# Attention with conditioned queries and keys on one core: how the quarters of the key sums are added

## The reference

```python
Q, K, V = heads(x @ Wq.T + bq), heads(x @ Wk.T + bk), heads(x @ Wv.T + bv)
tQ, tK  = heads(tokens @ Wq.T + bq), heads(tokens @ Wk.T + bk)
scores  = einsum('bhqd,bhkd->bhqk', Q + tQ, K + tK) / sqrt(32)
attn    = softmax(scores, axis=-1)
out     = x + merge(einsum('bhqk,bhkd->bhqd', attn, V))
```

## Time and profile before

| | us |
|---|---|
| median of 3 runs | 686.24 (685.55 to 686.38) |
| the profiled execution, its own time | 690.45 |
| its span, first to last instruction | 688.7 |
| PE busy in the span | 667.9 |
| DVE busy | 541.5 |
| POOL busy | 490.5 |
| ACT busy | 375.3 |

### The profile page before, as it was taken

One profiled execution on the slowest core, in us unless ns is written; L12 is line 12 of the kernel. 1 busy time (PEld: TensorE's weight loads), 2 busy tenths in 40 slices (PEclk: granted clock), 3 DMA queues, 4 the chain that ended last, 5 costly groups with the idle time before them and its releaser, 6 DMA issues.

```text
span 688.7 us, 10047 instructions
## 1 busy us (share of the span) xinstructions
PE 667.9 (97%) x3528; PEld 451.3 (66%) x3528; DVE 541.5 (79%) x818; ACT 375.3 (54%) x659; POOL 490.5 (71%) x205
## 2 busy tenths in 40 slices
PE   6899999999999999999999999999999999999986
PEld 4677766666776666677666666776666677665421
DVE  4386788888888888888888888888888888888736
ACT  6325655555565555565555565555555556556452
POOL 5506777788777778877777887777778776667780
PEclk9899999999999999999999999999999999999787
DMA  7924345553434555343455543434554333444111
GB/s 230 244 53 102 88 115 138 139 135 98 116 100 109 138 138 140 101 115 100 102 138 140 138 115 102 110 94 136 139 139 122 82 101 93 113 124 124 32 48 46
DMA packets 48274, 79.85 MB, mean 116 GB/s; under 512 B 9824, under 2 KB 9824, under 8 KB 48224
## 3 DMA queue, kind: packets, MB, share of 16 engines
q1 hardware_dynamic: 48224, 79.21, 43.2%
HBM read 19.95 MB, written 8.39 MB: 41 GB/s over the span
## 4 chain that ended last, share of the span: by engine, by line
PE 89%; DVE 3%; DMA 2%; issue 2%; SPq 1%; POOL 1%; POOLq 1%; ACT 1%; DVEq 0%; ACTq 0%
PE bank L193 24%; PE bank L262 18%; PE bank L277 17%; PE bank L292 15%; PE bank L240 13%; DVE mf L520 1%; PE bank L300 1%; DMA Ks<-lo 1%; DMA xr<-xT 1%; DVE part_sums L533 1%; POOL A L670 1%; POOLq L40 1%; DMA Pt<-xT 1%; PE bank L309 1%; SPq L722 1%
## 5 line engine op out<-in xcount | busy, mean ns | idle before, releaser
L439 ACT ACTIVATE Pt<-bank 128x512 f32<-128x512 f32 x512 | 301.2, 598 | 240.1 <-PE bank L277 157.7
L520 DVE TENSOR_REDUCE mf<-bank 128x1 f32<-128x512 f32 x512 | 344.6, 685 | 107.3 <-PE bank L262 106.2
L670 POOL TENSOR_TENSOR A<-A,Pt 128x2048 f32<-128x2048 f32 x62 | 284.4, 4588 | 4.9
L277 PE MATMUL bank<-Qs,Ks 98*128 98x512 f32 x512 | 212.4, 416 | 4.3 <-ACT Pt L439 2.5
L262 PE MATMUL bank<-Ks,Qs 96*128 96x512 f32 x512 | 210.1, 410 | 4.2 <-DVE mf L520 2.4
L670 POOL TENSOR_TENSOR A<-Pt 128x2048 f32<-128x2048 f32 x31 | 142.6, 4600 | 4.0 <-DVE part_sums L533 4.0
L277 PEld LDWEIGHTS bank<-Qs,Ks 98*128 98x128 f32 x512 | 97.6, 191 | 69.6 <-ACT Pt L439 46.1
L652 POOL TENSOR_TENSOR Xl<-xr,Xh 128x512 fp32r<-128x512 f32 x28 | 36.0, 1288 | 121.2 <-ACT Xh L407 121.2
L262 PEld LDWEIGHTS bank<-Ks,Qs 96*128 96x128 f32 x512 | 98.3, 192 | 31.4 <-DVE mf L520 6.2
L292 PE MATMUL bank<-Pt,V 128*32 128x512 f32 x992 | 115.4, 606 | 0.0
L193 PE MATMUL bank<-Xh,Wh 128*128 128x512 f32 x256 | 101.8, 398 | 0.8 <-DVE Wl L489 0.8
(11 more groups left out here) (52 smaller groups left out, 325.5 us busy)
## 6 DMA issues: line engine op xcount, KB each, us to landing
Qs<-hi SPq DMA_DIRECT2D x64, 256.0 KB, 3.6
Ks<-hi SPq DMA_DIRECT2D x64, 256.0 KB, 3.6
Qs<-lo SPq DMA_DIRECT2D x32, 256.0 KB, 4.1
Ks<-lo SPq DMA_DIRECT2D x32, 256.0 KB, 4.0
res<-xT SPq DMA_DIRECT2D x32, 256.0 KB, 2.9
outT<-ot SPq DMA_DIRECT2D x32, 256.0 KB, 3.5
xr<-xT SPq DMA_DIRECT2D x28, 256.0 KB, 2.7
Qs<-mt SPq DMA_DIRECT2D x128, 4.0 KB
```

The costliest lines, as they stand in the source:

```text
L277: e.matmul(STB[u % 2][:, :], Ks[0:98, sl, j, kc * P:(kc + 1) * P], Qs[0:98, sl, j, :], start=True, stop=True).then_inc(t_st, 1)
L439: e.activation(Pt[:, kc, j, :], STB[u % 2][:, :], ACT.Exp, scale=SCALE).then_inc(a_e, 1)
L520: e.reduce_max(mf[:, g % 2, 4 * j + qc:4 * j + qc + 1], MXB[u % 2][:, :], AXX).then_inc(v_mx, 1)
L670: e.tensor_tensor(A[:, :, :], Pt[:, 0, :, :] if kc == 1 else A[:, :, :], Pt[:, kc, :, :], ALU.add).then_inc(p_a, 1)
```

## The change

The matmuls of `totals` go. In their place SyncE writes `part_sums` to a scratch tensor in DRAM (`sums_out`, one DMA of 32 KB in 128 rows of 256 bytes), and reads it back with the quarters side by side (`sums_back`, four DMAs of 8 KB in 128 runs of 64 bytes each), so that partition 32 j + i holds the four partial sums of head j beside one another. VectorE adds them with one reduction of 64 numbers a partition (`quarters_added`) and takes the reciprocal (`totals_inverted`). These two stand in slot 15 of the stage before the one in which the reciprocal stood; the three other finishing steps keep their place in slot 1. FIN becomes 5. In SyncE's order `sums_out` stands behind the store and ahead of `maxima_rows`, `sums_back` behind `maxima_rows`. In the last stage group 30 is finished after the slots, behind the second of `last_adds`.

```diff
-FINISH_AT = (1, 1, 1, 1)
+FINISH_AT = (15, 15, 17, 17, 17)
-LAST_AT = (9, 10, 11, 12)
+LAST_AT = (9, 12, 15)
...
-            def totals(g, bk):
-                e.wait_ge(v_s, 2 * (g + 1))
-                for j in range(4):
-                    m = e.matmul(bk[32 * j:32 * j + 32, 0:16], sel[:, :], part_sums[:, j, :], start=True, stop=True)
-                m.then_inc(t_l, 1)
...
                     if n == VALUES_AT and t >= 1:
-                        if t >= 2:
-                            e.wait_ge(v_mx, min(u, SLOTS * G))
-                            totals(t - 2, MXB[(u + 1) % 2])
                         values(t - 1)
-                    if t == G - 1 and n == LAST_AT[0]:
-                        e.wait_ge(v_f, finished(G - 3, 1))
-                        totals(G - 2, MXB[0])
...
                     if g >= 1:
-                        e.wait_ge(t_l, g)
+                        e.wait_ge(d_ps, 16 * g)
...
-            def sums_inverted(g, bk):
-                e.wait_ge(t_l, g + 1)
-                if g >= 1:
-                    e.wait_ge(v_f, finished(g - 1, FIN))
-                e.reciprocal(rc[:, :], bk[:, 0:16]).then_inc(v_f, 1)
+            def quarters_added(g):
+                e.wait_ge(d_cb, 64 * (g + 1))
+                e.tensor_reduce(tot[:, :], comb[:, :, :].rearrange("p a n -> p n a"), AXX, ALU.add).then_inc(v_f, 1)
+
+            def totals_inverted(g):
+                e.wait_ge(v_f, finished(g, 1))
+                e.reciprocal(rc[:, :], tot[:, :]).then_inc(v_f, 1)
...
+            def sums_out(g):
+                e.wait_ge(v_s, 2 * (g + 1))
+                if g >= 1:
+                    e.wait_ge(d_cb, 64 * g)
+                e.dma_start(sums_dram.rearrange("a i j n -> (a i) (j n)"),
+                            part_sums[:, :, :].rearrange("p j n -> p (j n)")).then_inc(d_ps, 16)
+
+            def sums_back(g):
+                e.wait_ge(d_ps, 16 * (g + 1))
+                if g >= 1:
+                    e.wait_ge(v_f, finished(g - 1, 1))
+                for a in range(4):
+                    e.dma_start(comb[:, a, :], sums_dram[a].rearrange("i j n -> j i n")).then_inc(d_cb, 16)
...
                 if t >= 2:
                     store(t - 2)
+                if t >= 1:
+                    sums_out(t - 1)
                 if t + 1 < G:
                     maxima_rows(t + 1)
+                if t >= 1:
+                    sums_back(t - 1)
```

More of the change, by code:

```diff
@@ L20 @@
 SCALE = float(HD) ** -0.5
-FIN = 4
+FIN = 5
 MAX_LEAD = 9
@@ L72, in cond_attention @@
         cT = sb("cT", [P, KC, 32])
-        sel = sb("sel", [P, 32])
+        sel = sb("sel", [P, B])
         part_sums = sb("part_sums", [P, 4, 16])
+        comb = sb("comb", [P, 4, 16])
+        tot = sb("tot", [P, 16])
+        sums_dram = nc.dram_tensor("sums_dram", [4, 32, 4, 16], F32).ap()
         bqk = sb("bqk", [P, 3, KC])
@@ L91, in cond_attention @@
         d_mr = [sem(f"d_mr{i}") for i in range(2)]
+        d_ps = sem("d_ps")
+        d_cb = sem("d_cb")
         d_res = sem("d_res")
@@ L225, in condition_sum @@
                     m = e.matmul(OB[0][:, (qk * KC + c) * B:(qk * KC + c + 1) * B], part[qk][:, c * P:(c + 1) * P],
-                                 sel[:, 0:B], start=True, stop=True)
+                                 sel[:, :], start=True, stop=True)
                 m.then_inc(t_tb, 1)
@@ L249, in project, with maxima @@
                     project_qk("qk".index(kind), g, n)
-            def maxima(u, total=None):
+            def maxima(u):
                 g, m = divmod(u, SLOTS)
@@ L256, in maxima @@
                     e.wait_ge(v_mx, u - 1)
-                if total is not None:
-                    e.wait_ge(v_f, finished(total, 1))
                 if m == 0:
@@ L366, in tensor_program @@
                     if u < SLOTS * G:
-                        maxima(u, t - 2 if n == VALUES_AT + 1 and t >= 2 else None)
+                        maxima(u)
                     for k, g, i in work[done:done + PROJ[n]]:
@@ L372, in tensor_program @@
                     if n == VALUES_AT and t >= 1:
-                        if t >= 2:
-                            e.wait_ge(v_mx, min(u, SLOTS * G))
-                            totals(t - 2, MXB[(u + 1) % 2])
                         values(t - 1)
-                    if t == G - 1 and n == LAST_AT[0]:
-                        e.wait_ge(v_f, finished(G - 3, 1))
-                        totals(G - 2, MXB[0])
-                    if t == G - 1 and n == LAST_AT[3]:
+                    if t == G - 1 and n == LAST_AT[1]:
                         last_values(0)
@@ L556, in normalised @@
                 O = OB[g % 2]
-                e.wait_ge(v_f, finished(g, 2))
+                e.wait_ge(v_f, finished(g, 3))
                 if g < G - 1:
@@ L566, in added @@
                 c = g % KC
-                e.wait_ge(v_f, finished(g, 3))
+                e.wait_ge(v_f, finished(g, 4))
                 e.wait_ge(d_res, 16 * (g + 1))
@@ L615, in vector_program @@
                         qk_lo(0, g)
-                    if (g := due(t, n, FINISH_AT[0], -2)) is not None:
-                        sums_inverted(g, MXB[(SLOTS + VALUES_AT + 1 + MAX_LEAD) % 2])
-                    if (g := due(t, n, FINISH_AT[1], -2)) is not None:
+                    if (g := due(t, n, FINISH_AT[0], -1)) is not None:
+                        quarters_added(g)
+                    if (g := due(t, n, FINISH_AT[1], -1)) is not None:
+                        totals_inverted(g)
+                    if (g := due(t, n, FINISH_AT[2], -1)) is not None:
                         inverse_turned(g)
-                    if (g := due(t, n, FINISH_AT[2], -2)) is not None:
+                    if (g := due(t, n, FINISH_AT[3], -1)) is not None:
                         normalised(g)
-                    if (g := due(t, n, FINISH_AT[3], -2)) is not None:
+                    if (g := due(t, n, FINISH_AT[4], -1)) is not None:
                         added(g)
@@ L629, in vector_program @@
                         key_sums(g, 1)
[L630 to L641, removed]
+                    if t == G - 1 and n in (LAST_AT[0], LAST_AT[2]):
+                        last_adds(1 if n == LAST_AT[0] else 2)
+            inverse_turned(G - 2)
+            normalised(G - 2)
+            added(G - 2)
             last_sums_inverted()
```

8 lines of the change are left out of this document (4 added, 4 removed).

## The result

The changed kernel takes 688.75 us in the median of 9 runs (687.47 to 692.21), the kernel before 686.53 in 9 runs beside it. The ratio is 1.0035, 95% interval 1.0018 to 1.0052: slower by a third of a per cent. The prediction was 683.9 us and faster; the time lies in its range, but the direction is wrong.

What follows compares the result with a forecast made beforehand. PE, busy 97% of the span, was taken as the bound. Terms -4.2 (stages 2 to 28), -0.2 (stage 30), +0.5 (stage 29) and +1.55 (last stage) sum to -2.35 us: 683.9 us from 686.24, range 681.1 to 691.5.

Steps and rivals of the forecast that it cites:

- What the removal gives: PE, stages 2 to 28: dropping the totals matmuls saves 0.155 us a stage, 4.2 us over 27 stages.
- When the quarters are there: SP and DVE, slot 15: sums_back lands 2.1 us after its issue starts, so DVE stands 1.1 us.
- No stall, slack 0.2 us: K's last stack transfer: lands at 376.6, slot 7's tile wants it at 376.8, so PE does not wait.
- in time: The residual load, issued later in SP's queue, lands at 369.5, before DVE's use of it; no cost.
- The push back: SP's queue: x tile and residual start 2.7 us later, query transfers move from 365.5 to about 367.1; no stall.
- Rival 1: Quarters late, DVE's wait reaches PE at slot 4's tile and Ks<-lo: slower, for example 692.0 us; chance 0.27.
- The end: Stage 31: group 30's late finish delays the last residual and the last `added`, +1.55 us; stage 29 adds +0.5.
- The range: 8 in 10 for the whole kernel: 681.1 us to 691.5 us, the top from quarters landing late.

Runs made afterwards that it cites:

- no_totals: Kernel before without the totals matmuls and nothing in their place (reciprocal reads one head's partial sums, no adding of quarters); 680.22 us, ratio 0.9888.
- finish_late: Changed kernel with the sum of the quarters and the reciprocal moved from slot 15 to slot 1 of the next stage; 688.48 us, ratio 1.0004.
- after: The changed kernel itself, in its profiled execution, against the kernel before; median 688.75 us, ratio 1.0035.
- one_back_filler: Changed kernel with four short-run scratch writes, one wide read back, and five more such reads into unused tiles behind it; 696.22 us, ratio 1.0110.
- back_wide: Changed kernel with scratch laid out quarter, head, row, column: four writes, four 64-byte-run reads each over 128 rows in one dimension; 684.70 us, ratio 0.9958.
- block_late: Kernel before, no DMA added; SyncE waits for slot 15's maximum before issuing x tile, residual and stacks in stages 2 to 28; 692.71 us, ratio 1.0067.
- res_late: Kernel before with only the residual load moved behind SyncE's wait for the scores, directly ahead of the query stacks; 687.27 us, ratio 0.9997.
- dmas_only: Kernel before, totals kept, with the change's five small DMAs added in SyncE's order and their data unused; 689.83 us, ratio 1.0022.
- res_early: Changed kernel with the residual loaded right behind the previous store instead of behind sums_back; 683.95 us, ratio 0.9937.
- dmas_res_early: Kernel before plus the five unused small DMAs, with the residual loaded right behind the store; 688.04 us, ratio 1.0001.

## Why the prediction was wrong

- *What the removal gives*: right. 0.155 us a stage was forecast, 0.165 came, and the comparison with stage 1 gave the new stretch of 3.90 to the last digit. no_totals, with nothing in the place of the totals, has the same 19.83 in every steady stage.
- *When the quarters are there*: right. DVE's wait was forecast as 1.1 us and is 0.9 (0.26 us for the sum, against 0.25). SP's issues were cheaper than Qs<-mt's: 2.26 us for four, 0.33 for sums_out.
- *"No stall, slack 0.2 us" for Ks<-lo, and the residual "in time"*: this is the step that failed. The push back itself was forecast well (2.7 us for the loads, 2.6 measured), and so were the usual landings: 2.9 and 4.3 us were taken over from the kernel before, and the medians in the new block are 3.2 and 4.4. But a slack of 0.2 us was set against one usual landing. In the block the residual took up to 5.8 us where its slack was 1.3, and the K stack, forecast at 9.4 us behind the values' start, landed at 9.6 in the mean and at 10.5 at worst, at 9.4 or later in 15 of 25 stages. I had written that the push back "loads the queues" and then put its cost at nothing. The single late stages cost 6.0 us, more than the 4.3 that the removal gave.
- *Rival 1* named the right places on PE (slot 4's tile and Ks<-lo) and the wrong cause. The quarters were not late; finish_late took VectorE's wait for them away, and eight long stages and most of the loss stayed.
- *The end*: +1.85 us forecast with stage 29 and 30, -0.1 measured. The last `added` does wait for the residual (0.87 us), but sums_out landed in 1.4 us, not 2.3, and DVE's lag in stage 29 did not come: that stage took 17.76 us from values to values, the kernel before 18.15.
- *The range* took its upper part from rival 1. That it held the time is luck.

## What to carry to other kernels

When small DMAs are put into a queue, cost what they push back, not what they bring: the 64 KB out and back here had slack, the large transfers behind them had little. A usual landing time is no price where the slack is as small as its spread; take the slack of each pushed transfer against its slowest landing, and expect single stages to pay. The remedy was order and layout: loads that can go early go into the idle time of the queue, and the short runs of a rearrangement go on the side that has time.

## What the runs showed of the hardware

- A 256 KB load whose completions come from 16 engines can land on 15 of them in 3.0 us and on the last at 5.7. It did so in four traces, always with small reads issued directly ahead of the loads and the block late (after, finish_late, one_back_filler, and once in back_wide), and in the first three in the same few stages, 4, 14, 19 and 24. It did not in block_late, as late but with no small read ahead (at most 4.2 us), nor in res_late, where the stacks followed at once as well (3.4 us). In dmas_only, with the small reads, the worst was 4.2 us. Behind a store it landed in up to 4.6 us in res_early and 6.2 in dmas_res_early, at a time when nobody waited. What makes the one engine late stays open; the traces do not name the engine of a packet.
- Reading the same 8 KB with the same 64-byte runs costs SP 0.57 us from issue to issue when one side has the dimensions 4 x 32 and 0.44 when both have 128 (2.26 and 1.77 us for four); one read of 32 KB in 256-byte runs costs 0.35, and 0.43 for each of the five that follow it at once in one_back_filler.
- A group of eight 16-column matmuls on 32-column tiles, busy for 0.26 us, cost 0.165 us where a group on the same tiles followed. The Trainium skill's rule (TensorEngine Tiling (Array Packing), section Key Properties) that a change of tiling mode drains the array fits this: the first 32-column matmul starts 0.32 to 0.36 us behind the start of the projection ahead of it, with the group and without it, so the change of mode stays when the group goes.
